# Expert rows that carry half of the residual and are scattered plainly, with 36 first tiles and smaller moves around them

## The reference, cut to what matters

```
gate_logits = x @ W_gate                      # 8 per token
top_w, top_idx = top_k(gate_logits, 2); top_w = softmax(top_w)
h = gelu(x @ W_in[e] + b_in[e]);  y = h @ W_out[e] + b_out[e]
out = sum over the two experts of top_w * y;  x = layernorm(x + out)
```

## Time and profile before

| | us |
|---|---|
| median of 3 runs | 1401.18 (1400.07 to 1401.54) |
| profiled execution, device time | 1403.32 |
| its span in the trace | 1401.6 |
| PE busy | 1246.2 (89%) |
| DVE busy | 951.1 (68%) |
| ACT busy | 662.7 (47%) |
| POOL busy | 516.9 (37%) |

### The profile page before, as it was taken

One profiled execution on the slowest core, in us unless ns is written; L12 is line 12 of the kernel. 1 busy time (PEld: TensorE's weight loads), 2 busy tenths in 40 slices (PEclk: granted clock), 3 DMA queues, 4 the chain that ended last, 5 costly groups with the idle time before them and its releaser, 6 DMA issues. The chain is left out here.

```text
span 1401.6 us, 45150 instructions
## 1 busy us (share of the span) xinstructions
PE 1246.2 (89%) x16752; PEld 767.7 (55%) x16753; DVE 951.1 (68%) x2008; ACT 662.7 (47%) x1323; POOL 516.9 (37%) x509
## 2 busy tenths in 40 slices
PE   6679999999999987999999999999999985879990
PEld 3345444444444432446565655646565643779990
DVE  6667888778887853276776768586866657556664
ACT  3246667666766675242525243332525221335554
POOL 7402211122111121033443626153534425368785
PEclk9789999999999998999999999999999998979995
DMA  6453211221112222230403113130403032235545
GB/s 195 125 190 103 53 45 50 60 62 49 46 53 56 62 76 80 63 89 25 104 0 90 35 44 81 33 93 22 103 6 92 8 110 57 51 60 73 66 57 188
DMA packets 95017, 100.02 MB, mean 71 GB/s; under 512 B 16096, under 2 KB 76640, under 8 KB 94752
## 3 DMA queue, kind: packets, MB, share of 16 engines
q1 hardware_dynamic: 75936, 81.72, 21.2%
q0 software_dynamic: 13568, 12.13, 5.6%
q10 hardware_dynamic: 5376, 4.20, 0.9%
HBM read 49.83 MB, written 27.87 MB: 55 GB/s over the span
## 5 line engine op out<-in xcount | busy, mean ns | idle before, releaser
L1635 DVE TENSOR_REDUCE arena<-banks 128x4 f32<-128x512 f32 (+3 forms) x336 | 343.4, 1066 | 92.8 <-PE banks L1404 88.4
L1570 ACT ACTIVATE arena<-banks 128x512 f32<-128x512 f32 x576 | 304.9, 603 | 165.6 <-PE banks L1404 160.5
L1404 PE MATMUL banks<-arena 99*32 99x512 bf16 (+7 forms) x6144 | 335.0, 330 | 31.4 <-DVE arena L1635 12.6
L1404 PEld LDWEIGHTS banks<-arena 96*32 96x32 bf16 (+1 forms) x6144 | 150.2, 96 | 191.5 <-ACT arena L1570 69.8
L481 PE MATMUL banks<-arena,h 128*128 128x512 f32 x512 | 226.7, 593 | 2.4 <-DVEq L407 1.0
L1772 POOL TENSOR_SCALAR_AFFINE_SELECT arena<-arena 128x512 f32<-128x512 f32 x128 | 79.9, 637 | 381.5 <-ACT arena L1570 368.4
L1471 PE MATMUL banks<-arena 128*32 128x512 f32 (+3 forms) x1536 | 153.7, 490 | 11.2 <-POOL arena L1772 11.0
L481 PEld LDWEIGHTS banks<-arena,h 128*128 128x128 f32 x512 | 94.7, 190 | 110.0 <-issue 105.2
L635 ACT ACTIVATE arena<-banks,sh 128x512 f32<-128x512 f32 x64 | 44.0, 687 | 215.3 <-PE banks L481 215.3
L1066 POOL DMA_INDIRECT best<-arena x72 | 116.3, 1615 | 41.4 <-issue 22.8
L497 POOL TENSOR_TENSOR arena<-arena 128x4 f32<-128x4 f32 x23 | 23.4, 1017 | 267.0 <-DVE arena L495 267.0
(11 more groups left out here) (196 smaller groups left out, 1775.4 us busy)
## 6 DMA issues: line engine op xcount, KB each, us to landing
arena<-arena SPq DMA_DIRECT2D x160, 128.0 KB, 2.3
arena<-k_parts SPq DMA_DIRECT2D x96, 96.0 KB
arena<-rows SPq DMA_DIRECT2D x72, 65.0 KB, 2.1
arena<-q_parts SPq DMA_DIRECT2D x64, 64.0 KB
k_parts<-arena SPq DMA_DIRECT2D x24, 128.0 KB, 3.5
q_parts<-arena POOLq DMA_DIRECT2D x24, 128.0 KB, 3.2
arena<-q_parts SPq DMA_DIRECT2D x32, 96.0 KB
best<-arena SPq DMA_DIRECT2D x12, 256.0 KB, 3.0
```

The source lines that it names most:

```text
L1404: ins = nc.tensor.matmul(dst[c:c + 32, :], lhs[:, c:c + 32], rhs, start=start, stop=stop, skip_group_check=True)
L1570: nc.scalar.activation(pe_[:, s % NSLOT, :], score[s % NBANK], ACT.Exp, scale=SCALE0)\
L1635: nc.vector.tensor_reduce(mx[:, 1 if k0 else 0, qt, hs[0]:hs[-1] + 1], src, AX.X, ALU.max)\
```

## The change

- `layernorm` gets a factor: the third one writes 0.5 of x3 (variance scaled by 4 before the power). What reads it is corrected: the logits are multiplied by 2 as DVE takes them from PSUM, the gelu of the experts gets `scale=2.0`.
- Each of the two expert rows of a token adds its 0.5 of x3: the bias step becomes a `scalar_tensor_tensor` (bias times weight plus the row's x3), reads the bias out of `w_in` directly, is done inside `take_w` (2 ahead, three buffers), and `weigh` is gone. `take_w` copies 512 columns.
- So `best` needs neither a residual nor zeros: the transfer "stored", the zeroing transfers and the waits for them are gone, and `back` scatters plainly.
- `NTILE` is 71, `AHEAD` is 36: tiles 4 to 35 are straight code, 36 to 59 loop, 60 to 70 straight.
- For tiles below 36 `take_x` is done by ACT, behind the gelu of its slot.
- The steps of `plan_table` run in pairs among pass 8 (four pairs behind the `mul` steps L554, three between the attention steps, three behind the layernorm); those of `tile_table` run in pairs, one pair behind each slot from 5. The wait between two steps now stands ahead of the later one.
- The exponential of the gap is a power of e on POOL; the three DVE steps behind it move to `shares`, behind slot 3.

```diff
-NTILE = TOPK * NT // P + NE
+NTILE = (TOPK * NT + NE * (P - 1)) // P
-AHEAD = 24
+AHEAD = 36
...
-                var[:, :], mv[:, :, 1], EPS, None, ALU.add))
+                var[:, :], mv[:, :, 1], EPS, share ** -2, ALU.add, ALU.mult))
...
+            def plan():
+                next(planned, None)
+                next(planned, None)
...
-            tp.do("act", "stored", ["norm3"], lambda: nc.scalar.dma_start(
-                plain_v[bass.ds(c, 1)].rearrange("c p b k -> p (c b) k"), x3), line="out")
...
-                tp.do("act", "exp", ["gap"], lambda: nc.scalar.activation(wgt[:, 1, :], expd, ACT.Exp))
+                tp.do("pool", "exp", ["gap"], lambda: nc.gpsimd.tensor_tensor(
+                    wgt[:, 1, :], euler[:, :], expd, ALU.pow))
...
                 def take_x(J, k):
-                    e.wait_ge(s_tp, XG * J + k + 1)
-                    wait(s_up, XG * J + k - 3)
-                    nc.vector.tensor_copy(x_gT[:, k % 4, :], banks[:, k % 2, 0:P]).then_inc(s_xt, 1)
+                    j = XG * J + k
+                    early = isinstance(j, int) and j < AHEAD
+                    if isinstance(j, int) and j == AHEAD:
+                        e.wait_ge(s_xt, AHEAD)
+                    e.wait_ge(s_tp, j + 1)
+                    wait(s_up, j - 3)
+                    (nc.scalar.copy if early else nc.vector.tensor_copy)(
+                        x_gT[:, k % 4, :], banks[:, k % 2, 0:P]).then_inc(s_xt, 1)
...
+                    e.wait_ge(s_xg[k], 16 * (J + 1))
+                    wait(s_y, XG * J + k - 2)
+                    nc.vector.scalar_tensor_tensor(
+                        out=bias[:, k % 3, :], in0=w_in[:, bass.ds(x, 1), 512:512 + C].rearrange("p o m -> p (o m)"),
+                        scalar=x_g[:, k, C + 1:C + 2], in1=x_g[:, k, 0:C], op0=ALU.mult, op1=ALU.add).then_inc(s_bias, 1)
...
-                def weigh(J, k):
-                    e.wait_ge(s_xg[k], 16 * (J + 1))
-                    e.wait_ge(s_w1, XG * J + k + 1)
-                    wait(s_y, XG * J + k - 1)
...
-                        in_=y_g[:, k, :], in_offset=None, compute_op=ALU.add).then_inc(s_back[k], 16)
+                        in_=y_g[:, k, :], in_offset=None).then_inc(s_back[k], 16)
...
-                chain = {"sp": [(load, XG)], "pe": [(turn, 3), (up, 1), (down, 0)], "act": [(gelu, 0)],
-                         "dve": [(take_x, 3), (take_w, 2), (weigh, 1), (take_y, 0)], "pool": [(back, 0)]}[me]
+                chain = {"sp": [(load, XG)], "pe": [(turn, 3), (up, 1), (down, 0)], "act": [(gelu, 0), (take_x, 3)],
+                         "dve": [(take_x, 3), (take_w, 2), (take_y, 0)], "pool": [(back, 0)]}[me]
...
-                if j in (5, 7, 9):
+                if j > 4:
+                    next(table_parts, None)
                     next(table_parts, None)
...
-                if isinstance(u, int) and u in (1, NU - 2):
-                    clear(u > 1)
```

178 lines of the change are left out of this document (130 added, 48 removed).

## The result

| | kernel before | changed kernel |
|---|---|---|
| median of 8 runs each, us | 1399.21 (1396.09 to 1401.54) | 1393.43 (1389.98 to 1396.16) |
| ratio, 95% interval | | 0.9956 [0.9941, 0.9971] |
| profiled execution, us (span) | 1403.32 (1401.6) | 1393.33 (1390.7) |

The account below looks back on a forecast made before the run. PE was taken as the bound, with some 18 us to gain in one weak stretch. Terms +1.6 - 4.5 - 3.0 - 7.5 - 1.3 - 1.9 - 1.6 = -18.2 us gave 1383.0 us; 8-in-10 range 1374 to 1393.

Parts of the forecast that it names:

- What bounds the kernel: PE bounds passes and steady tiles; some 18 us to be had between 1197 and 1236 us, hardly anything elsewhere.
- The passes: Routing passes: exponential and table loads leave ACT, but were covered by its wait for DVE; 0 us a pass.
- The plan: Pass 8: steps spread ahead of work PE waits for, at the first scores; +1.6 us, bounds 0 to 3.9.
- slower: All 71 tiles: bias step or ACT's copy lengthens each from 1.91 to 2.45 us, giving 1421 us; chance 0.05.
- The block at tile 3: Pass 9 to tile 3: PE's wait for the gelu and the slow product go; -4.5 us, bounds -2.5 and -5.9.
- Tiles 3 to 5: Two slots plus shares and routing on DVE take 5.8 instead of 8.8 us; -3.0 us, bounds -1 and -4.
- Tiles 5 to 16: Slots of 2.1 us on DVE, half the late signals coming again; -7.5 us, bounds 0 and -12.
- Tiles 16 to 36: Twelve tiles leave the hardware loop, 1.91 us a tile; -1.3 us, bounds +1 and -1.5.
- The rest of the tiles: After tile 36: one tile less, other loop turns as before; -1.9 us.
- The plain scatter at the end: Behind the last tile: queue goes and the scatter is shorter; -1.6 us, bounds -0.5 and -2.8.
- The start: Base time from which the forecast's gains were subtracted, 1401.18 us, 2.1 us below the profiled execution.
- DVE takes over: Tiles 3 to 16: DVE slots cost 2.7 instead of 2.1 us, 8 us return, giving 1391 us; chance 0.20.

Follow-up runs that it names:

- second pair: Kernel before and changed kernel, both unchanged, profiled once more on a faster chip; spans 1387.6 and 1372.8 us.
- e3: Changed kernel with the exponential of the gate on ScalarE again; 1382.59 us, ratio 0.9944 to the kernel before.
- e4: Kernel before with only the exponential moved to GpSimd and the shares computed behind tile 3's slot; 1387.82 us, ratio 0.9983.
- f3: Changed kernel with the copies of the turned rows on VectorE again for all tiles; 1379.57 us, ratio 0.9931.
- f2: Changed kernel, unchanged, profiled again on a faster chip; 1378.23 us, ratio 0.9922 to the kernel before.
- i3: Kernel before with a plain scatter of the expert rows alone, on a faster chip; 1389.74 us, ratio 0.9992.
- g1: Kernel before with a plain scatter of the expert rows alone, on a slower chip; 1407.59 against 1402.16 us, ratio 1.0040.
- h2: Changed kernel with seven scatters spaced behind every second tile and the plan in one piece, on a slower chip; 1391.13 us, ratio 0.9928.
- e2: Changed kernel with seven of the last routing's eight scatters spaced behind every second tile, on a faster chip; 1373.57 us, ratio 0.9879.

## Why the prediction was wrong, step by step

The step that failed most is the term of tiles 5 to 16: -7.5 us forecast, with half of the late signals gone, and -2.1 us measured, since none of them went. Apart from the start, the first pair lacks 10.5 us of the 18.2: 5.4 there, 2.1 at the end, 1.5 in tiles 16 to 36, 1.2 in the plan, 1.0 in tiles 3 to 5, and under 1 us in the rest, against 1.5 us more than forecast at tile 3. In the second pair tiles 5 to 16 came as forecast, and the step that failed most is tiles 16 to 36.

*What bounds the kernel.* Right. All that moved by over 0.4 us, apart from the start, moved in pass 8 or behind it.

*The passes.* Right: five passes +0.3 us in both pairs, and e3 shows the loads covered. The 43 us that the Trainium skill's figures would have made of them (ScalarE: Activation LUTs, What ACT_TABLE_LOAD costs) are not there. On the path at tile 3 its figure for the load fits (1.28 us), its 1380 ns for a drain at each switch does not: in e3 the gelu starts 0.01 us behind its load, and ahead of the load only 0.49 us are idle.

*The plan.* +1.6 forecast, +1.1 and +2.8 measured. The place was wrong: PE's wait at the first scores did not grow (0.95 and 0.96 us in the first pair, 0.34 and 0.35 in the second), it waited 2.0 us at a later mask step. I had priced the steps at 0.28 us from where GpSimd was idle; beside its state update they take 0.76 to 0.95 us. The port pair that I had weighed for the bias step shows here, if anywhere. The bias step itself took 0.33 to 0.40 us in all tiles (median 0.35), beside scatters too, so the rival "slower" falls.

*The block at tile 3.* Right in the main: -4.5 forecast, -4.6 in the second pair, 4.9 when undone (e3). In the first pair -6.0. That the size fits so well is in part luck: alone in the kernel before the step is worth 3.0 us there (e4), and ACT's copies, for which I had put nothing, 1.2 us (f3).

*Tiles 3 to 5.* Wrong in size. I took the 8.8 us of the first trace as the kernel's; in the second trace of the same kernel they are 5.8. Of -3.0 us, -2.0 and -0.3 were there.

*Tiles 5 to 16.* The slot was right (2.1 us each, 23.1 us forecast, 22.99 measured in the second pair). That the difference fits too, -7.5 and -7.3, is luck: the kernel before has no late signals there and takes 30.3 us instead of 34.4, which stands in for the 3.8 us that I let come again. The term failed on the first chip by the one part that I could not explain and halved. The late signals came back in full and more, 10.8 us, and the measured -2.1 us is below the bound that would have followed from that (-11.3 + 7.5 = -3.8). They are there on all three slower chips and on none of the three faster ones, so no reading of one trace could have said whether to count them.

*Tiles 16 to 36.* Wrong: -1.3 forecast, +2.7 in the second pair. I had not asked what the faster tiles would demand of the queues of GpSimd and SP, that is, whether the rows of tiles 20 to 22 would still be there in time. On the first chip the gap at tile 6 hides this, and late signals at every second tile between 27 and 35 (2.7 and 1.4 us in turn) take its place.

*The rest of the tiles.* -1.9 forecast, -1.4 and -3.3 measured. The second has 1.90 us in the loop instead of 1.95, which I had not counted. The first lost 2.2 us in two tiles (3.53 and 2.47 us, tiles 51 to 53).

*The plain scatter at the end.* Wrong: -1.6 forecast, +0.5 and +0.2 measured. The chain of the changed kernel's first trace:

```profile
1356.26 0.36 DVE arena L1073
1356.66 0.74 issue
1357.40 0.94 POOL best L1080
1358.34 0.74 issue
1359.08 2.97 DMA best<-arena
```

I had read the 1.77 us between `take_y` and transfer as queue. In a kernel without queue it is 2.46 us: 0.74 before the instruction, 0.94 for it, 0.74 behind it. 

*The start.* The base was a median of three runs, 1401.18 us. Eight give 1399.21, which alone moves a forecast of 1383.0 to 1381.0.

*The rivals.* "DVE takes over" gave 1391, nearest to what came, for a wrong reason: DVE set only a few slots of the changed kernel, by 0.4 us each (tiles 7, 10 and 13 of f2 take 2.3 us, where `take_w` comes behind steps of the table and PE's product starts 0.1 us after it). As a difference the forecast's range was -27 to -8 us; -12.1 on the faster chip lies in it, -5.8 does not. The range had no case in which the unexplained stall grows.

## What to carry to other kernels

Where a stretch of a trace has time that no instruction explains, take a second trace before counting any of it as gain, on another chip if there is one. When the work between two queues gets faster, follow the buffers round the ring (here scatter, load, turn, twelve tiles on) and ask which queue is now late. Price a small vector step by rows taken beside the same neighbours that it will have: 0.18 us alone was 0.76 to 0.95 us beside GpSimd's elementwise work.

## What the runs showed of the hardware

The chips differ in a way that changes what an edit is worth: plain scatters in the kernel before gained 1 us or nothing on one kind (i3) and lost 5.4 on the other (g1), spacing the scatters gained 5 us in tiles 3 to 36 on the one (70.9 us in f2, 65.7 in e2), and on the other only moved the stall (h2). Signals of TensorE came up to 10 us behind the recorded end of a product while GpSimd sent plain indirect scatters of 0.96 us back to back, and only on the slower chips; adding ones of 1.6 us at the same distance held nothing up on either kind. One wait of 2.0 us cost either that alone or another 1.6 us, as the clock fell behind it or not (products of 1.99 us against 1.09 us).
